# A decoder layer on one core: three weight splits move to GpSimd, a normalisation and a transpose group move later, and the last scratch write becomes one

## The reference, cut to what matters

```python
# 1. recurrent block
n = layernorm(x);  u = n @ Wi.T + bi;  g = sigmoid(n @ Wg.T + bg)
h[t] = g[t] * h[t-1] + (1 - g[t]) * u[t]          # along the 100 tokens
x = x + h @ Wo.T + bo
# 2. cross attention, 8 heads of 128; keys are 722 context rows + 100 latents
q = ln(x) @ Wq + bq;  k, v = split([ln(ctx), ln(x)] @ Wkv + bkv)
x = x + softmax(q @ k.T * 128**-0.5) @ v @ Wo_x + bo_x
# 3. top-1 mixture of 8 experts, 512 -> 2048 -> 512, exact gelu
x = x + max_prob * sum_e mask_e * (gelu(ln(x) @ W1[e]) @ W2[e])
```

## Time and profile before

| what | value |
|---|---|
| median of 3 runs | 1116.23 us |
| the profiled execution, and its span | 1115.66 us, 1113.8 us |
| TensorE busy | 1043.4 us (94%) |
| VectorE, ScalarE, GpSimd busy | 768.9 us (69%), 561.1 us (50%), 146.0 us (13%) |
| the chain that ended last, by engine | PE 69%, DVE 13%, issue 6%, DMA 5%, ACT 4%, POOL 2% |

### The profile page before, as it was taken

How to read it: one execution, slowest core, us unless ns; L and a number is a source line. 1 busy time by engine, 2 the same in 40 slices (tenths; PEclk the granted TensorE clock), 3 DMA queues, 4 the chain that set the end, 5 groups by cost and what they waited for, 6 DMA issues and landing times.

```text
span 1113.8 us, 18444 instructions
## 1 busy us (share of the span) xinstructions
PE 1043.4 (94%) x6264; PEld 953.2 (86%) x6265; DVE 768.9 (69%) x1345; ACT 561.1 (50%) x1123; POOL 146.0 (13%) x134
## 2 busy tenths in 40 slices
PE   4899999999999999999999999999975999999996
PEld 4878897999999999999999999987954878887775
DVE  7778545866858669587695875675667965857981
ACT  4424555354444544445444454572543855846871
POOL 4407320000000000000000000001011221311341
PEclk9999999999999999999999999999985999999998
DMA  9221857113031130311303103368355992955960
GB/s 314 60 80 56 296 178 284 46 60 121 4 130 52 59 119 4 125 58 59 118 5 125 57 0 132 116 232 307 104 158 171 341 327 100 346 205 200 356 245 30
DMA packets 82037, 160.98 MB, mean 145 GB/s; under 512 B 12605, under 2 KB 29501, under 8 KB 80080
## 3 DMA queue, kind: packets, MB, share of 16 engines
q1 hardware_dynamic: 80240, 155.70, 39.9%
q0 software_dynamic: 1760, 4.79, 1.2%
HBM read 127.68 MB, written 33.78 MB: 145 GB/s over the span
## 4 chain that ended last, share of the span: by engine, by line
PE 69%; DVE 13%; issue 6%; DMA 5%; ACT 4%; POOL 2%; DVEq 0%; SPq 0%; POOLq 0%; ACTq 0%
PE bank L583 20%; PE bank L585 19%; PE bank L584 19%; PE bank L1060 3%; PE bank L1026 2%; DMA stage<-in_W 2%; DMA gat<-scr_tokens,idc 2%; DVE xn_l L1471 2%; DVE wsl L1471 1%; PE bank L1078 1%; PE bank L1047 1%; PE bank L1045 1%; PE bank L1077 1%; ACT wsh L1333 1%; PE bank L1184 1%
## 5 line engine op out<-in xcount | busy, mean ns | idle before, releaser
L583 PE MATMUL bank<-pt_h,xn_h 128*128 128x256 f32 (+1 forms) x576 | 170.4, 296 | 6.9 <-DVE pt_l L1471 6.9
L585 PE MATMUL bank<-pt_h,xn_l 128*128 128x256 f32 (+1 forms) x576 | 164.8, 286 | 0.0
L584 PE MATMUL bank<-pt_l,xn_h 128*128 128x256 f32 (+1 forms) x576 | 164.7, 286 | 0.0
L1471 DVE TENSOR_TENSOR wsl<-stage,wsh 128x2048 fp32r<-128x2048 f32 x64 | 145.6, 2289 | 21.9 <-ACT wsh L1333 19.4
L583 PE MATMUL bank<-xt_h,qt_h 128*128 128x410 f32 (+1 forms) x384 | 136.5, 355 | 5.6 <-ACT pr L1287 5.6
L1333 ACT CAST wsh<-stage 128x2048 fp32r<-128x2048 f32 x64 | 122.5, 1916 | 27.5 <-DMA stage<-in_W 15.7
L584 PE MATMUL bank<-xt_l,qt_h 128*128 128x410 f32 (+1 forms) x384 | 134.1, 349 | 0.0
L585 PE MATMUL bank<-xt_h,qt_l 128*128 128x410 f32 (+1 forms) x384 | 134.1, 349 | 0.0
L583 PEld LDWEIGHTS bank<-pt_h,xn_h 128*128 128x128 f32 x576 | 108.8, 189 | 9.5 <-issue 7.1
L1284 ACT ACTIVATE pr<-bank,smx 128x412 f32<-128x412 f32 x48 | 29.1, 606 | 162.0 <-DVE smx L1627 162.0
L584 PEld LDWEIGHTS bank<-pt_l,xn_h 128*128 128x128 f32 x576 | 109.0, 189 | 0.0
(11 more groups left out here) (238 smaller groups left out, 2541.7 us busy)
## 6 DMA issues: line engine op xcount, KB each, us to landing
stage<-in_W SPq DMA_DIRECT2D x64, 1024.0 KB, 7.3
scr_q<-st SPq DMA_DIRECT2D x16, 800.0 KB, 4.9
qf<-scr_q SPq DMA_DIRECT2D x8, 1600.0 KB, 6.7
zr<-scr_z SPq DMA_DIRECT2D x16, 800.0 KB, 5.4
scr_z<-zf SPq DMA_DIRECT2D x7, 1600.0 KB, 5.3
raw<-in_ctx SPq DMA_DIRECT2D x8, 768.0 KB, 4.5
raw<-in_ctx SPq DMA_DIRECT2D x8, 512.0 KB
wq<-in_Wq SPq DMA_DIRECT2D x1, 2048.0 KB, 17.4
```

The costliest lines, as they stand in the source:

```text
L583: pe.matmul(dest, lh, rh, start=start and k == 0, stop=False)
L584: pe.matmul(dest, lh, rl, start=False, stop=False)
L585: last = pe.matmul(dest, ll, rh, start=False, stop=stop and k == n - 1)
L1471: return dve.tensor_tensor(dst, src, high.bitcast(F32), ALU.subtract)
```

## The change

Nine edits:

1. SyncE issues WiT ahead of x 4 to 7 instead of behind them.
2. `low_weight(2)`, `(3)` and `(4)`, subtractions of 128 x 2048, are done by GpSimd instead of VectorE, behind the eight `xin` adds: (2), (3), the inverse deviations of the context (`rows_std(0)`), (4). TensorE waits for a semaphore of its own (`s_wil`).
3. The three `bkm` instructions move on VectorE from behind the layernorms to ahead of the scan loop.
4. `rows_norm(0, 0)`, six instructions, moves on VectorE from the loop's turn e = 1 to behind the layernorms, in front of `rows_norm(0, 1)`.
5. `by_act`: in the first half, VectorE takes blocks 1 and 3 of the heads 2 to 7 (12 units) instead of block 3 of the heads 3 to 7 (5 units).
6. Latents 4 to 7 are transposed together behind head 7 of the first half, instead of one behind each of the heads 4 to 7; ScalarE's and VectorE's parts move with them.
7. The last batch's Z is written by one transfer of 1600 KB when all is there, ahead of `load_unit(4)`, instead of 1000 KB early and 600 KB behind it.
8. The expert's first two weight pieces are loaded between `load_unit(6)` and `load_unit(7)` instead of behind `load_unit(12)`.
9. TensorE's wait for `s_ce` = 2 moves from behind the first batch's opening events to the end of `queries`.

```diff
@@ which engine takes out a unit
-    by_act = [what == "q" or dc % 2 == 0 or (half, h) < (0, 3) or half == 0 and dc < 3 for what, half, h, dc in q_units]
+    by_act = [what == "q" or dc % 2 == 0 or (half, h) < (0, 2) for what, half, h, dc in q_units]
@@ sync
+            load_w3(0)
             load_x(range(HALF, B))
-            load_w3(0)
             load_w3(1)
...
-            for k in range(2):
-                sp.wait_ge(s_zread[k], (B - 1) * (ZB_USES // 2) + ND + 1)
-            sp.dma_start(d_z[B - 1][:, 0:whole], flat[:, 0:whole]).then_inc(s_zd, 16)
-            for k in range(2):
-                sp.wait_ge(s_zread[k], B * (ZB_USES // 2) + 1)
+            write_z(B - 1)
             load_unit(4)
-            sp.dma_start(d_z[B - 1][:, whole:HEADS * ND * T], flat[:, whole:HEADS * ND * T]).then_inc(s_zd, 16)
-            reload_units(range(5, 8))
-            sp.wait_ge(s_zd, 16 * (B + 2))
+            reload_units(range(5, 7))
+            load_weights(0, 0, range(2))
+            reload_units(range(7, 8))
+            sp.wait_ge(s_zd, 16 * (B + 1))
             reload_units(range(8, 13))
-            load_weights(0, 0, range(4))
+            load_weights(0, 0, range(2, 4))
@@ gpsimd
+            def low_weight(k):
+
+                pool.wait_ge(s_wah, k + 1)
+                pool.tensor_tensor(weights_a(k, w3_l, wq_l), weights_a(k, w3, wq), weights_a(k, w3_h, wq_h).bitcast(F32),
+                                   ALU.subtract).then_inc(s_wil, 1)
...
+            low_weight(2)
+            low_weight(3)
             rows_std(0)
-
+            low_weight(4)
@@ tensor
-            pe.wait_ge(s_wal, 3)
+            pe.wait_ge(s_wil, 1)
...
-            pe.wait_ge(s_wal, 5)
...
+            pe.wait_ge(s_wil, 3)
...
-                    if not half and h >= HALF:
-                        latents([h])
                 if not half:
+                    latents(1)
                     pe.wait_ge(s_x1, B)
...
+                pe.wait_ge(s_ce, 2)
                 for u in range(len(q_units) - 4, len(q_units)):
                     free_unit(pe, u)
...
             run(0, rest)
-            pe.wait_ge(s_ce, 2)
@@ vector
             low_weight(1)
-            low_weight(2)
+            dve.wait_ge(s_ca, 16 * N_CA)
+            ch.add(dve.tensor_tensor(bkm[:], bkm[:], bk[:].unsqueeze(2).broadcast_to([P, HEADS, HEADS]), ALU.mult))
...
+            tally(s_bkm)
...
                 if e == 0:
                     rows_stats(0, 0)
                     rows_stats(0, 1)
-                    low_weight(3)
-                elif e == 1:
-                    rows_norm(0, 0)
-                elif e == 2:
-                    low_weight(4)
...
+            rows_norm(0, 0)
             rows_norm(0, 1)
```

More of the change, by code:

```diff
@@ L381, in build @@
     s_id, s_wk = sem("s_id"), sem("s_wk")
+    s_wil = sem("s_wil")
     s_ca, s_wq, s_cc, s_zout = sem("s_ca"), sem("s_wq"), sem("s_cc"), sem("s_zout")
@@ L767, in _ @@
             load_unit(3)
-            whole = (GROUPS[1][-1] + 1) * P // T * ND * T
-            flat = zf[:].rearrange("p h c t -> p (h c t)")
-            for k in range(2):
-                sp.wait_ge(s_zread[k], (B - 1) * (ZB_USES // 2) + ND + 1)
-            sp.dma_start(d_z[B - 1][:, 0:whole], flat[:, 0:whole]).then_inc(s_zd, 16)
-            for k in range(2):
-                sp.wait_ge(s_zread[k], B * (ZB_USES // 2) + 1)
+            write_z(B - 1)
             load_unit(4)
-            sp.dma_start(d_z[B - 1][:, whole:HEADS * ND * T], flat[:, whole:HEADS * ND * T]).then_inc(s_zd, 16)
-            reload_units(range(5, 8))
-            sp.wait_ge(s_zd, 16 * (B + 2))
+            reload_units(range(5, 7))
+            load_weights(0, 0, range(2))
+            reload_units(range(7, 8))
+            sp.wait_ge(s_zd, 16 * (B + 1))
             reload_units(range(8, 13))
-            load_weights(0, 0, range(4))
+            load_weights(0, 0, range(2, 4))
             for b in range(HALF):
@@ L952, in _, with latents @@
                     last.then_inc(s_op, 1)
-            pe.wait_ge(s_wal, 5)
-            def latents(bs):
-                for b in bs:
+            pe.wait_ge(s_wil, 3)
+            def latents(half):
+                for bb in range(HALF):
+                    b = half * HALF + bb
                     pe.wait_ge(s_lnr, b + 1)
@@ L1133, in batch @@
                 steps(run, b, events)
-            latents(range(HALF))
+            latents(0)
             queries(run)
@@ L1238, in _, with latents @@
                 act.copy(wk_h[:, 4 * k:4 * k + 4, :], wk[:, 4 * k:4 * k + 4, :]).then_inc(s_wkh, 1)
-            def latents(bs):
-                for b in bs:
+            def latents(half):
+                for b in range(half * HALF, (half + 1) * HALF):
                     act.wait_ge(s_tpl, b + 1)
@@ L1380, in _ @@
                     run(0, early.get((half, h), []))
-                    if not half and h >= HALF:
-                        latents([h])
                 if (what, h, dc) == ("k", HEADS - 1, ND - 1):
+                    if not half:
+                        latents(1)
                     act.wait_ge(s_cp, half + 1)
@@ L1475, in low_weight @@
                 dve.wait_ge(s_wah, k + 1)
-                low(weights_a(k, w3_l, wq_l), weights_a(k, w3, wq), weights_a(k, w3_h, wq_h)).then_inc(s_wal, 1)
+                low(w3_l[k][:], w3[k][:], w3_h[k][:]).then_inc(s_wal, 1)
             def low_rows(b, n, src, done):
@@ L1514, in _ @@
             low_weight(1)
-            low_weight(2)
+            dve.wait_ge(s_ca, 16 * N_CA)
+            ch.add(dve.tensor_tensor(bkm[:], bkm[:], bk[:].unsqueeze(2).broadcast_to([P, HEADS, HEADS]), ALU.mult))
+            ch.join()
+            ch.add(dve.tensor_copy(bkm_h[:], bkm[:]))
+            ch.join()
+            ch.add(low(bkm_l[:], bkm[:], bkm_h[:]))
+            tally(s_bkm)
             for e in range(ND):
@@ L1693, in finish @@
                         else:
-                            dve.wait_ge(s_zd, 16 * (B + 2))
+                            dve.wait_ge(s_zd, 16 * (B + 1))
                         ch.add(dve.tensor_tensor(x2b[b % 2][0:T, :], zbank[b % 2][0:T, :], x1b[b % 2][0:T, :], ALU.add))
@@ L1740, in _ @@
                         run(0, early.get((half, h), []))
-                        if not half and h >= HALF:
-                            low_rows(h, B + h, tbank[h % 2], s_tel)
+                        if (half, h) == (0, HEADS - 1):
+                            for b in range(HALF, B):
+                                low_rows(b, B + b, tbank[b % 2], s_tel)
             dve.wait_ge(s_cp, 2)
```

## The result

The changed kernel takes 1134.7 us (median, 1133.0 to 1136.7) against 1116.4 us of the kernel before in the same session; the ratio is 1.0163, 95% interval 1.0143 to 1.0182. Its profiled execution took 1135.27 us, with a span of 1133.5 us. Slower was right, 1136.4 us was 1.7 us too much, and the range held the time. But one of its terms, 0.2 us, measured 4.2 us, and most of the others erred the other way.

What follows compares the result with a forecast made beforehand. TensorE, busy 94% of the span, was taken as the bound, so edits count through its stops and clock. 2.0 + 9.0 + 1.1 + 8.6 = 20.7 us on 1115.66 gave 1136.4 us; 8-in-10 range 1128.5 to 1143.

Steps and rivals of the forecast that it cites:

- Edit 1: At the start: statistics of x 4 to 7 could wait for the last row, 0.2 us (0 to 0.5).
- Loop: Recurrent block: VectorE and GpSimd hold each other up; +2.0 us including 0.2 for WiT's early issue, ends -5.7 and +4.5.
- GpSimd's rate: Loop: a GpSimd subtraction of 2048 elements takes 4.8 us, between 4.6 by slope and 5.1 in proportion.
- `og` slips in: Loop, turn 0: `og` runs before the first long GpSimd instruction; `u * og` and the scan wait, +3.4 us.
- Keys: Keys: VectorE's first unit 3.7 us later and wanted 3.3 us earlier, plus 2 us of clock; +9.0 us.
- Latents together: Latents behind head 7: two buffers serve four latents, so the third and fourth wait; +1.1 us, ends 0 and +1.6.
- Values: Last units: queue order delays unit 7, +6.6 us, plus 2 us for the clock; +8.6 us.
- Edit 9: Around the first batch's scores: the moved wait is covered by the 2.33 us stop at 190.49; nothing, 0.7 without cover.
- A: Rival up to the keys: VectorE's relief is not held up by GpSimd, saving 8.4 us; 1107.3 to 1115.9 us; 5%.
- B: Rival at the values: transfers on the queue run side by side, tail costs 2 us; 1129.8 us; 15%.
- C: Rival at keys and tail: `bkm`'s time comes back, neither long stop slows the clock; 1130.6 us; 12%.
- D: Rival: long GpSimd instructions take 5.1 us and collide each time, clock loses 3 us twice; 1142.7 us; 14%.

Runs made afterwards that it cites:

- e2: The changed kernel with WiT issued behind x 4 to 7 again; ratio 1.0140 to the kernel before.
- e3: Kernel before, with only the first normalisation put behind the loop and the new split of q and k units; 1127.7 us, ratio 1.0089.
- e4: Kernel before, with only Z written whole ahead of unit 4 and two weight pieces loaded between units 6 and 7; ratio 1.0075.
- e5: Kernel before, with only the three low weight parts moved to GpSimd; ratio 1.0056.
- e6: Kernel before, with only the two weight pieces loaded between units 6 and 7 of Z; ratio 1.0065.
- e7: Kernel before, with only TensorE's wait for ScalarE's last c8 moved to before it frees the last units; ratio 0.9991.
- e10: Kernel before, with only the last batch's Z written whole ahead of unit 4; ratio 1.0039.
- e9: Kernel before, with WiT issued early and rows 4 to 7 of x issued on ScalarE's queue at the start; ratio 1.0035.
- e12: Kernel before, with ScalarE taking out all units of heads 0 to 3 of the first half, and the c8 wait moved; ratio 0.9957.

## Why the prediction was right, and where it was not

- **Edit 1 (0.2 us predicted, 0 to 0.5): the failed step.** I took the statistics "without a wait" at 11.44 and let them wait for the last row for 0.5 us at most. But 1 MB ahead in the same queue puts that row from 10.9 to 17.4 us. Measured 4.2 us in after, 2.6 (0.7 to 4.6) in time. It should have been costed by the bytes ahead, like edit 8, and even that falls short: 1.05 MB at the 294 GB/s of this stretch (8 to 18 us) is 3.6 us, not 6.5. What the rest is, no run here shows. That the sum fitted is luck: +4.0 us here stand against -1.6 in the loop, -0.8 in keys and latents, -0.7 by edit 9, -1.6 in the values and -0.3 behind them.
- **Loop (1.8 without edit 1).** Measured 0.2 in after, 0.6 in e2. GpSimd's rate was right: 4.56 to 4.62 us for 2048 elements, the slope's 4.6 and not the 4.8 I took. Right also: the first stop of about 4 us (3.96), the second small (it is gone). Wrong: "`og` slips in". It stood 4.77 us beside the first long instruction, and the scan, at 1.82, beside none; the earlier trace rows had shown `og` only where it came first. I had used the rule of the Trainium skill (SBUF — State Buffer, "Who interferes with whom") without its exception: an instruction with one input stays out only outside the modes that use both ports, and `tensor_scalar` can have such a mode. The traces agree with both halves, the statistics (3.65 us for six, unhindered) and `og`; which mode `og` ran in, they do not show.
- **Keys (+9.0: 7.0 and 2 of clock).** From the output projection to the same matmul as 122.21 in before: 8.3 us in after, 9.1 in e2, 9.8 in e3. In after VectorE's first unit came at 129.15, 3.1 us later than before once the 4.4 us of start and loop are taken off (3.7 predicted); in e3, where `bkm` stays, 4.0, so moving `bkm` gave back 0.9 us and not 0.4. The stop was 10.57 us (9.7), and the clock cost 2 us. That this makes 8.3 and not 9.9 has its reason in before, told below: there TensorE came late to its stop, in after it did not.
- **Latents together (+1.1).** Measured 1.06 us in after and in e2, over the matmuls from 122.21 to 130.53, and none in e3, which lacks edit 6. Edit 6 was not run by itself.
- **Values (+8.6: 6.6 and 2 of clock).** 7.0, 8.5 and 9.6 us in three traces (after, e4, e2). Unit 7's matmuls began where predicted, once the earlier delay is taken off: 773.87 - 13.05 = 760.8 (759.6 to 761.2). In after the clock fell behind the first stop only.
- **Edit 9 (nothing).** It gains about 1 us: the chain over ScalarE that I thought it leaves alone does begin earlier.
- **Rivals.** A: relief is held up, as e5 shows. B: the queue is in order. C came closest in its sum of the tail, by the clock, but not at the keys. D's two clock losses of 3 us were not seen in after.

The base also had luck in it. TensorE's time from 60 to 122 us does not count, since VectorE sets the end of that stretch. Where the clock fell at 90 to 94 us, as in before and e6, TensorE came late to the stop, found it 2.67 us long, and went on at full clock. Where it did not fall, as in e7 and e10, it found a stop of 4.2 us, and the clock fell there: 1.5 to 1.6 us that count in e7, e9 and e10, 3.0 in e4, by the columns up to 130.53. Busy time by stretch, before and then e10:

```profile
90.00:94.00 4.00, 4.00 (x15) 4.00 (x15) 3.29 (x8) 0.50 (x2) 1.23 (x3) 0.59 0.36 114
...
122.00:126.00 4.00, 3.79 (x25) 3.70 (x26) 1.64 (x4) 2.06 (x5) 0.00 (x0) 1.00 0.96 344
```
```profile
90.00:94.00 4.00, 3.17 (x17) 3.17 (x18) 3.60 (x8) 0.78 (x3) 1.47 (x2) 1.00 0.51 152
...
122.00:126.00 4.00, 2.78 (x10) 2.65 (x11) 1.92 (x5) 0.50 (x1) 0.00 (x0) 0.64 0.61 225
```

Four of the eight traces with before's keys (e4, e7, e9, e10) went that way. It can explain part of before's scatter of 1113.3 to 1123.1 us; this was not tested by itself.

## What to carry to other kernels

Where a load is issued ahead of others in one queue, count its bytes at the measured rate onto each load behind it, at the start of the kernel too, and look who waits for the last of them. At the end of this kernel that gave the delay (5.4 us), at its start too little (3.6 of 6.5 us). Another queue, in the one trial here, changed who was late and not how much was moved. Find the engine that sets the end of a stretch: here VectorE up to the first `st` unit, so an instruction moved there costs in full, and a unit taken from it gains. Work handed to GpSimd is not gone from VectorE; which VectorE instruction stands beside it decided here between 0 and 4 us.

## What the runs showed of the hardware

- GpSimd: 4.56 to 4.62 us for 128x2048 f32 `tensor_tensor`, 4.93 to 4.95 where VectorE was busy first; VectorE takes 2.28.
- Beside it a VectorE `tensor_scalar` of 0.57 us took 4.77, three normalisation instructions 6.42 instead of 2.07; six BATCH_NORM_STATS2 took their 3.65.
- The length of a stop did not tell by itself whether the clock would fall: behind 2.99 us in e4 (at 54 us) it stayed at 1.00, behind 2.98 us in before (at 53) and 1.77 us in e12 it fell to 0.50.
- 2.10 MB issued between two loads on one queue put their casts 7.53, 7.53, 7.53 and 7.54 us apart in four kernels (after, e2, e4, e6), instead of 2.1; with two queues in use at the start, row 3 of x came 2.0 to 2.9 us later.
- From the issue of a 13 KB write to what waits for it: 1.5 us in the five traces with edit 9, 2.5 to 3.2 us in the nine without; the cause is open.
- Code that no edit touched ran with the clock low at 90 to 94 us in some executions and not in others; by that the stop at 122 us was 2.7 or 4.2 us long, and the clock behind it 1.00 or down to 0.50.
